# A mixture-of-experts block loop: the output bias added on VectorE straight from PSUM, the gate and the gelu's high part on ScalarE, GpSimd's hold instructions taken out

## The reference, cut to what matters

```
h = gelu(einsum('bsd,edh->bseh', x, w1) + b1)         # d = 512, h = 256
expert_out = einsum('bseh,ehd->bsed', h, w2) + b2
out = einsum('bse,bsed->bsd', gates, expert_out)      # gates: softmax of the two best experts, else 0
x = x + tanh(g_ffn) * out
```

## Time and profile before

| | |
|---|---|
| median of 3 runs | 2121.07 us (2115.35 to 2128.86) |
| the profiled execution | 2121.86 us |
| its span, first to last instruction | 2119.7 us |
| mean granted TensorE clock | 0.965 of 2.4 GHz |
| block loop, second gelu of the first block to that of the last | 1557.67 to 2106.64 us, 36 periods |

### The profile page before, as it was taken

The page is one execution under the profiler, slowest core; times in us unless marked ns, Lnnn a source line. Parts: engine busy times, 40 slices in busy tenths (PEclk is TensorE's granted clock), DMA queues, the critical chain, the costliest instruction groups (busy, mean ns, idle before and its releaser), DMA issues. The chain is left out here.

```text
span 2119.7 us, 38741 instructions
## 1 busy us (share of the span) xinstructions
PE 1891.6 (89%) x10720; PEld 1050.8 (50%) x10721; DVE 1565.7 (74%) x3713; ACT 1096.3 (52%) x1970; POOL 715.6 (34%) x547
## 2 busy tenths in 40 slices
PE   0599999999999999999999999999379899998987
PEld 0344444444444444444444444443257677676765
DVE  6577788777877878877777787874467677766775
ACT  0155555556656555565655656565244444454443
POOL 1112111111111101111111111100068888888887
PEclk9999999999999999999999999999589999999999
DMA  3877677667777777777677686763358786877784
GB/s 110 137 116 154 114 182 143 129 152 122 184 142 130 162 115 182 145 134 160 123 168 145 128 170 123 148 129 106 100 114 148 146 143 130 153 135 134 131 155 69
DMA packets 173114, 292.01 MB, mean 138 GB/s; under 512 B 37982, under 2 KB 42078, under 8 KB 172944
## 3 DMA queue, kind: packets, MB, share of 16 engines
q1 hardware_dynamic: 140016, 222.26, 51.6%
q0 software_dynamic: 32928, 67.68, 18.2%
HBM read 127.09 MB, written 71.63 MB: 94 GB/s over the span
## 5 line engine op out<-in xcount | busy, mean ns | idle before, releaser
L918 DVE TENSOR_REDUCE mx<-bank 128x1 f32<-128x512 f32 x1024 | 692.3, 685 | 239.4 <-PE bank L714 220.8
L622 ACT ACTIVATE prob<-bank 128x512 f32<-128x512 f32 x1024 | 578.5, 595 | 491.8 <-PE bank L702 491.7
L590 POOL TENSOR_TENSOR regrouped_then_w<-regrouped_then_w 128x512 fp32r<-128x512 f32 x128 | 164.8, 1287 | 1145.8 <-ACT regrouped_then_w L612 1145.8
L714 PE MATMUL bank<-stA,stB 98*128 98x512 f32 x1024 | 428.9, 421 | 66.6 <-DVE mx L918 41.7
L702 PE MATMUL bank<-stB,stA 100*128 100x512 f32 x1024 | 469.0, 460 | 8.7 <-issue 8.4
L702 PEld LDWEIGHTS bank<-stB,stA 100*128 100x128 f32 x1024 | 196.8, 193 | 212.1 <-ACT prob L622 113.3
L675 PE MATMUL bank<-prob,vin 128*32 128x512 f32 x2048 | 281.2, 622 | 0.0
L675 PE MATMUL bank<-prob,ones 128*32 128x512 f32 x2048 | 277.8, 615 | 0.0
L1153 POOL DMA_INDIRECT rows_in<-xn_rows,gather_ids x152 | 207.8, 1367 | 162.5 <-DVE rows_in L1363 121.1
L714 PEld LDWEIGHTS bank<-stA,stB 98*128 98x128 f32 x1024 | 202.8, 198 | 113.4 <-DVE mx L918 73.2
L1183 POOL DMA_INDIRECT out_dram<-yout,scatter_ids x144 | 238.1, 1653 | 40.4 <-issue 35.9
(11 more groups left out here) (184 smaller groups left out, 2170.5 us busy)
## 6 DMA issues: line engine op xcount, KB each, us to landing
stB<-regrouped_then_w SPq DMA_DIRECT2D x192, 256.0 KB, 5.7
stA<-regrouped_then_w SPq DMA_DIRECT2D x192, 256.0 KB, 8.3
x_k_then_w<-in_x_dram SPq DMA_DIRECT2D x16, 1024.0 KB, 6.3
x_k_then_w<-in_ctx_dram SPq DMA_DIRECT2D x16, 1024.0 KB, 8.6
vin<-in_ctx_dram SPq DMA_DIRECT2D x16, 1024.0 KB, 6.4
xres<-in_x_dram SPq DMA_DIRECT2D x16, 1024.0 KB, 12.5
xn_rows<-xn SPq DMA_DIRECT2D x64, 256.0 KB, 2.3
out_dram<-xres SPq DMA_DIRECT2D x16, 1024.0 KB, 10.8
```

The costliest lines, as they stand in the source:

```text
L590: pool.tensor_tensor(turnedL[:, side, :], turned[:, side, :], turnedH[:, side, :].bitcast(F32), ALU.subtract).then_inc(s_lo, 1)
L622: act.activation(prob[:, u % 2, j, :], psS[j % 2][:, :], ACT.Exp).then_inc(s_exp, 1)
L714: pe.matmul(psM[s % 2][:, :], stB[0:98, g, j, i * P:(i + 1) * P], stA[0:98, g, j, :], start=True, stop=True).then_inc(s_m, 1)
L918: dve.tensor_reduce(mx[:, s // 4, s % 4:s % 4 + 1], psM[s % 2][:, :], AX.X, ALU.max).then_inc(s_mx, 1)
```

## The change

- VectorE adds `b2` to the product as it lies in PSUM (`psY` + `b2s` into `ysum`); ScalarE then multiplies by the gate, from `ysum` in SBUF into `yout`. Before, ScalarE gated first and VectorE added gate times bias.
- The high part of the gelu is copied by ScalarE and no longer by VectorE. Both copies stand **behind both gelus** in ScalarE's program. VectorE is left with the two subtractions.
- GpSimd's two holds are gone. VectorE waits on the landed scatters (`f_add`) before it copies the scatter ids; ScalarE waits on the landed scatters of two blocks back before it writes `yout`; `pool.sem_inc(f_go, 1)` stands where the holds were.
- One more empty indirect DMA is issued ahead of the loop.

```
@@ gpsimd step
-                        pool.wait_ge(f_hold, st.rnd * 4 + 2 * h)
                         pool.wait_ge(f_use, st.steps(USES, -1, 2 + USES))
                         pool.wait_ge(f_gate, st.steps(1, -1, 1))
-                        carry_wait()
+                        pool.sem_inc(f_go, 1)
                         gather(st.par(1))
-                        pool.wait_ge(f_hold, st.rnd * 4 + (2 * h + 1))
-                        pool.wait_ge(f_add[1 - h], st.rnd * (16 * NS) + (0 if h else 16 - 16 * NS))
+                        pool.wait_ge(f_add[1 - h], added(st, 1))
                         pool.wait_ge(f_yo, st.back(NS, 0, NS))
-                        carry_wait()
+                        pool.sem_inc(f_go, 1)
@@ tensor second
-                        pe.wait_ge(f_hs, st.front(2 * KE, -1, 2 * m + 2))
+                        pe.wait_ge(f_hs, st.front(KE, -1, m + 1))
@@ scalar step
+                            act.wait_ge(f_add[st.h], added(st, 2))
                             for c in range(NS):
-                                act.wait_ge(f_y, st.back(NS, 0, c + 1))
-                                act.wait_ge(f_yo, st.back(NS, -1, c + 1))
-                                act.activation(ysum[:, c, :], psY[c][:, :], ACT.Copy, scale=gate[:, st.h, c:c + 1]).then_inc(f_yg, 1)
+                                act.wait_ge(f_yg, st.back(NS, 0, c + 1))
+                                act.activation(yout[:, st.h, c, :], ysum[:, c, :], ACT.Copy, scale=gate[:, st.h, c:c + 1]).then_inc(f_yo, 1)
                         for m in range(KE):
                             act.wait_ge(f_h, st.front(KE, 0, m + 1))
                             ...
                             act.activation(gelu[:, m, :], psH[m][:, :], ACT.Gelu, bias=b1s[:, st.par(), m:m + 1]).then_inc(f_g, 1)
+                        for m in range(KE):
+                            act.wait_ge(f_g, st.front(KE, 0, m + 1))
+                            act.activation(hT[:, 0, m, :], gelu[:, m, :], ACT.Copy).then_inc(f_hhi, 1)
@@ vector step
+                        if not st.first:
+                            dve.wait_ge(f_yo, st.back(NS, -1, NS))
                         dve.tensor_scalar(gate[:, st.par(), :], ...).then_inc(f_gate, 1)
                         if not st.first:
                             dve.wait_ge(f_b2[st.h], st.rnd * 16)
-                            dve.wait_ge(f_hold, st.rnd * 4 + 2 * st.h)
                             for c in range(NS):
-                                dve.wait_ge(f_yg, st.back(NS, 0, c + 1))
-                                dve.scalar_tensor_tensor(out=yout[:, st.h, c, :], in0=b2s[:, st.h, :], scalar=gate[:, st.h, c:c + 1],
-                                                         in1=ysum[:, c, :], op0=ALU.mult, op1=ALU.add).then_inc(f_yo, 1)
+                                dve.wait_ge(f_y, st.back(NS, 0, c + 1))
+                                dve.tensor_tensor(ysum[:, c, :], psY[c][:, :], b2s[:, st.h, :], ALU.add).then_inc(f_yg, 1)
                         if not st.first:
-                            dve.wait_ge(f_hold, st.rnd * 4 + (2 * st.h + 2))
+                            dve.wait_ge(f_add[1 - st.h], added(st, 1))
                         dve.tensor_copy(sids[:, st.par(), :], gids[:, st.par(), :]).then_inc(f_sid, 1)
                         ...
                         for m in range(KE):
-                            dve.wait_ge(f_g, st.front(KE, 0, m + 1))
-                            dve.tensor_copy(hT[:, 0, m, :], gelu[:, m, :]).then_inc(f_hs, 1)
-                            dve.wait_ge(f_hs, st.front(2 * KE, 0, 2 * m + 1))
+                            dve.wait_ge(f_hhi, st.front(KE, 0, m + 1))
                             dve.tensor_tensor(hT[:, 1, m, :], gelu[:, m, :], hT[:, 0, m, :].bitcast(F32), ALU.subtract).then_inc(f_hs, 1)
```

More of the change, by code:

```diff
@@ L1046, in flamingo_kernel @@
             hT = sb("gelu_parts", [P, 2, KE, BLK], F32R)
-            ysum = sb("out_gated_rows", [P, NS, D])
+            ysum = sb("out_with_bias", [P, NS, D])
             yout = sb("yout", [P, 2, NS, D])
@@ L1068, in flamingo_kernel @@
             f_g = sem("gelu_done")
+            f_hhi = sem("gelu_hi")
             f_hs = sem("gelu_split")
             f_y = sem("out_ready")
-            f_yg = sem("out_gated")
+            f_yg = sem("out_biased")
             f_yo = sem("out_done")
-            f_hold = sem("pool_held")
+            f_go = sem("pool_goes_on")
             f_clear = sem("rows_cleared")
-            adds = [(f_y, 2 * NS), (f_yg, 2 * NS), (f_yo, 2 * NS), (f_hold, 4)]
+            adds = [(f_y, 2 * NS), (f_yg, 2 * NS), (f_yo, 2 * NS)]
             with nc.Block() as block:
@@ L1116, in split_product, with added @@
                 return last
+            def added(st, back):
+                return st.rnd * (16 * NS) + (16 if back == 1 and st.h else 16 - 16 * NS)
             with nc.Block() as block:
@@ L1147, in _ @@
                 def _(pool):
-                    def carry_wait():
-                        pool.tensor_tensor(hold[:, 5:6], ones[:, 0:1], ones[:, 0:1], ALU.add).then_inc(f_hold, 1)
                     def gather(par):
@@ L1162, in step @@
                                 gather(i)
-                            pool.indirect_dma_start(nowhere_d, bass.IndirectOffsetOnAxis(ap=nowhere[:, 0:1], axis=0),
-                                                    nothing[:, :], None, bounds_check=P - 1,
-                                                    oob_is_err=False).then_inc(f_add[1], 16)
+                            for i in range(2):
+                                pool.indirect_dma_start(nowhere_d, bass.IndirectOffsetOnAxis(ap=nowhere[:, 0:1], axis=0),
+                                                        nothing[:, :], None, bounds_check=P - 1,
+                                                        oob_is_err=False).then_inc(f_add[i], 16)
                             return
                         h = st.h
-                        pool.wait_ge(f_hold, st.rnd * 4 + 2 * h)
                         pool.wait_ge(f_use, st.steps(USES, -1, 2 + USES))
                         pool.wait_ge(f_gate, st.steps(1, -1, 1))
-                        carry_wait()
+                        pool.sem_inc(f_go, 1)
                         gather(st.par(1))
-                        pool.wait_ge(f_hold, st.rnd * 4 + (2 * h + 1))
-                        pool.wait_ge(f_add[1 - h], st.rnd * (16 * NS) + (0 if h else 16 - 16 * NS))
+                        pool.wait_ge(f_add[1 - h], added(st, 1))
                         pool.wait_ge(f_yo, st.back(NS, 0, NS))
-                        carry_wait()
+                        pool.sem_inc(f_go, 1)
                         for c in range(NS):
@@ L1189, in _ @@
                     n = n_rounds(pool)
-                    pool.wait_ge(f_add[0], n * (16 * NS))
+                    pool.wait_ge(f_add[0], n * (16 * NS) + 16)
                     pool.wait_ge(f_add[1], n * (16 * NS) + 16)
@@ L1290, in step @@
                             if not st.first:
-                                act.wait_ge(f_hs, st.front(2 * KE, -1, 2 * m + 2))
+                                act.wait_ge(f_hs, st.front(KE, -1, m + 1))
                             act.activation(gelu[:, m, :], psH[m][:, :], ACT.Gelu, bias=b1s[:, st.par(), m:m + 1]).then_inc(f_g, 1)
+                        for m in range(KE):
+                            act.wait_ge(f_g, st.front(KE, 0, m + 1))
+                            act.activation(hT[:, 0, m, :], gelu[:, m, :], ACT.Copy).then_inc(f_hhi, 1)
                     act.wait_ge(s_w, 16 * 2 * E)
```

## The result

The changed kernel takes 2109.03 us (median of 11 runs, 2100.22 to 2117.65) against 2124.02 (11 runs): ratio **0.9933**, 95% interval 0.9917 to 0.9950, some 14 us less. I had put it at 2119 with "no change" as the likeliest case; it lies in the range of 2100 to 2142 and within 1%, but it is faster clear of noise.

What follows compares the result with a forecast made beforehand. The prediction took GpSimd as the bound, its relief eaten by a longer ring: 1.88 + 2.10 + 0.47 + 10.80 = 15.25 us a period, unchanged, and 2.5 us off the tail, 2121.9 to 2119.4, taken as 2119 us; range 2100 to 2142.

Steps and rivals of the forecast that it cites:

- three signs of being wrong: Block loop: low part outside 1.75 to 2.13 us after second gelu's start, clock below 0.97, or first gelu awaiting gates.
- GpSimd is full and sets the pace: Block loop before the change: GpSimd's 462 us busy plus 78 us issue idle fill 540 of 549 us.
- clean ring: Undisturbed period through ScalarE, VectorE and TensorE: 14.55 us, against a mean period of 15.25 us.
- The holds, 1.6 us a step: GpSimd in the block loop: 71 holds take 56 us, 1.6 us a step, which the change removes.
- The stretched gather beside yout: GpSimd's second gather, beside yout operations reading two SBUF tensors: 2.65 us against 1.09; the change ends the stall.
- The gelu's high part costs the ring: ScalarE's copies behind both gelus: second low part 1.88 us after second gelu's start, formerly 1.18 clean, 1.65 on average.
- The sum, 15.25 us a period: New period in the block loop: 1.88 + 2.10 + 0.47 + 10.80 = 15.25 us, same as the mean before.
- late periods: Periods where GpSimd has fallen behind: low part 2.2 to 2.35 us after second gelu's start, in 14 of 36.
- second(0) hides under VectorE by 0.3 us: TensorE: second(0) ends 4.9 us after second gelu's start, before VectorE releases turn 2 at 5.17 us.
- the first: Rival: copies cost the ring nothing, every period is clean, 28 us less, 2094 us; chance 0.10.
- the second: Rival: TensorE's idling lowers its clock, 2180 us if every period, 2139 if one of three; chance 0.12.
- the third: Rival: scatters landing in over 8.0 us set the period; at 8.5 us, 16 us more, 2135 us; chance 0.06.

Runs made afterwards that it cites:

- yout_psum: Kernel before, with VectorE's four yout operations reading the second tensor from the product's PSUM bank, gate left out of the product: 0.9872 of before, 14.48 us a period.
- holds_out: Kernel before with only GpSimd's holds taken out; bias, gate and the gelu's high part as before: 1.0021 of before, 15.24 us a period.
- bias_only: Kernel before with only bias and gate swapped between VectorE and ScalarE, holds kept, high part on VectorE: 0.9913 of before, 14.72 us a period.
- holds_bias: Changed kernel with the gelu's high part back on VectorE; holds out, bias and gate swapped: 0.9921 of before, 14.75 us a period.
- late: Changed kernel with VectorE's two register loads and L1312 moved behind the low parts of pieces 0 and 1: 0.9929 of before, 14.86 us a period.
- sbuf_add: Changed kernel with the high part back on VectorE, whose four additions read b2s twice instead of product and b2s: 1.0027 of before, 15.48 us a period.

## Why the prediction was half right

The forecast was 36 x 0.00 in the loop and -2.5 us in the tail; the profiles show -11.4 and -2.0. None of the three signs of being wrong turned up: the low part starts at T+1.85, the granted clock is 1.00, and ScalarE's first gelu waits for TensorE. The new ring was the right mechanism, and one term of it was too large. That the sum came to exactly the mean of before, "no change", was a coincidence of two different bounds.

**GpSimd is full and sets the pace**: right. Shown by yout_psum, which keeps the order of the work and shortens what GpSimd does (gathers from 1.36 to 1.15 us, holds from 0.79 to 0.52): 14.48 us, where I had 14.55 for the clean ring. That they meet so closely is partly luck: the low part started at T+1.35 in the mean, not 1.18, and the loads behind it took 1.88 us, not 2.10.

**The holds, 1.6 us a step**: wrong. I took their busy time for work that would be saved. Of the 56 us, 20 lay over the scatter before the hold, so I had counted them twice: the three groups of the earlier trace rows sum to 481.6 us, and GpSimd's busy time in the earlier trace rows is 461.8. In holds_out the gathers then take 16 us more, the scatters 10 more, and the idle time put down to "issue" grows by 15. Nothing is left: 0.00 us a period.

**The stretched gather beside yout**: right in cause, and the whole of the relief: -0.53 us a period by itself (bias_only), where I had treated it as an addition to the holds. I gave gathers 1.09 us, they took 1.13.

**The gelu's high part costs the ring**: right in direction and place. The second low part was to start at T+1.88 and did at T+1.85; TensorE was to idle 1.2 us ahead of second(0) and idled 1.32 in the mean. It cost 0.18 us a period against holds_bias by the profiles, and 0.65, clear of noise, with late loads.

**The sum, 15.25 us a period**: the term that was mis-sized is the 2.10 us of register loads between low part and L1312, carried over from before. They measured 1.83 us. 0.27 of the 0.32 us that the period was too long is this term; the rest is 0.03 at the low part and 0.02 behind L1307. I had argued that in late periods "the register loads did not shrink" and took them as fixed. They are not, and the trace of before already said so: over its 14 late periods the distance from low part to L1309 is 2.04 us in the mean, over the 16 with the low part at T+1.18 it is 2.22. I had read one late period, with one of the longest. About 0.1 us is the queue (the second low part is now issued while the first still runs, so the loads start with it and no longer 0.1 us after), the rest shorter loads, 0.41 instead of 0.48 us each, two a step. Why they are shorter is open. Two readings were off without touching the sum: the other 22 periods have their low part at up to T+1.67, not 1.5, and the last four scatters issue in 7.38 us by the earlier trace rows, not 7.2.

**second(0) hides under VectorE by 0.3 us**: wrong in consequence; with the shorter loads the two are tied near 14.86, and late shows the ring through second(0) as the floor.

**Cover of ScalarE's gates, 1 us**: right, 0.99 to 1.14 us idle ahead of the first gelu. **Tail**: -2.5 predicted, -2.0 measured; scatters start at T-2.9, not T-3.7, since nearly 1 us passes between the last gate and the first scatter.

**Rivals**: the first (relief in full, 28 us) is what the swap without the copies goes two thirds of the way to, 18 us in bias_only; the second (clock) did not occur, no period over 15.28 us; the third (scatters' chain) did not either, GpSimd waits for yout, not for landed scatters.

## What to carry to other kernels

An engine that is full is not always relieved by taking its own instructions out. Look first at which of its instructions are stretched and what runs beside them, since a stall can move to the next instruction when the one that carried it goes; and compare the sum of the groups with the engine's busy time, since instructions can overlap. For the indirect gathers on GpSimd here the cause was VectorE's operations with two SBUF inputs, and giving one input from PSUM was the cure. Before moving a copy to a less busy engine, ask which instruction it will then stand behind. Treat register loads at the head of a loop step as a term that varies, and read it from all periods.

## What the runs showed of the hardware that I had not expected

- Moving one operand of VectorE's four 128x512 operations between SBUF and PSUM changed the kernel by 1.1 to 1.3%: gathers of 1.36 against 1.15 us in the mean (before, yout_psum) and of 1.54 against 1.22 us (sbuf_add, holds_bias).
- VectorE's register load took 0.30 us alone and up to 1.11 us beside a scatter that GpSimd was issuing; nearly all the long ones lay there.
- A one-element GpSimd operation took 0.21 us behind a gather and 1.39 us in the mean behind a scatter, 0.55 of it over the scatter's own time.
- An additional register load cost 0.97 us a period, three times the 0.30 that a load takes alone.
